# Four layers of graph attention on one core: layer 3 with stacked key terms, a one-pass leaky maximum, another step of lag, two copies on VectorE and a reordered step

## What is computed

```python
x = _layernorm(x + layer(x, adj))      # four times, another layer each time
```

```python
Wh = (h @ W).reshape(b, n, H, HD).transpose(0, 2, 1, 3)
e1 = jnp.einsum('bhnd,d->bhn', Wh, a1)
e2 = jnp.einsum('bhnd,d->bhn', Wh, a2)
e = e1[:, :, :, None] + e2[:, :, None, :]
e = jnp.where(adj_mask == 0, -jnp.inf, e)
e = jnp.where(e >= 0, e, 0.2 * e)
attn = jax.nn.softmax(e, axis=-1)
h_prime = jnp.einsum('bhij,bhjd->bhid', attn, Wh)
```

## Time and profile before

| | us |
|---|---|
| median of 3 runs | 723.36 (722.78 to 723.52) |
| profiled execution | 720.54 |
| its span, first to last instruction | 718.7 |
| TensorE busy | 653.0 (91%) |
| VectorE busy | 600.8 (84%) |
| ScalarE busy | 539.4 (75%) |
| GpSimd busy | 512.9 (71%) |

### The profile page before, as it was taken

One profiled execution on the slowest core, in us unless ns is written; L12 is line 12 of the kernel. 1 busy time (PEld: TensorE's weight loads), 2 busy tenths in 40 slices (PEclk: granted clock), 3 DMA queues, 4 the chain that ended last, 5 costly groups with the idle time before them and its releaser, 6 DMA issues.

```text
span 718.7 us, 17483 instructions
## 1 busy us (share of the span) xinstructions
PE 653.0 (91%) x6378; PEld 489.9 (68%) x6378; DVE 600.8 (84%) x1515; ACT 539.4 (75%) x852; POOL 512.9 (71%) x541
## 2 busy tenths in 40 slices
PE   3999799998799999999999998799999999999972
PEld 2888577776456666666666666676777777777751
DVE  4799679998778888988898886798888888888872
ACT  1555589987478777787777776588899899899882
POOL 6477559999675677767777765467776777767785
PEclk9999999999589999999999999999999999999996
DMA  9900000000000000000000000000100000100001
GB/s 255 279 3 1 2 0 1 2 1 2 0 1 2 3 1 2 1 2 1 2 2 2 2 1 2 1 2 1 31 16 16 16 17 16 31 16 16 16 16 44
DMA packets 28897, 14.91 MB, mean 21 GB/s; under 512 B 1926, under 2 KB 28812, under 8 KB 28812
## 3 DMA queue, kind: packets, MB, share of 16 engines
q1 hardware_dynamic: 25344, 12.59, 6.8%
q10 hardware_dynamic: 3468, 1.20, 0.8%
HBM read 9.59 MB, written 4.19 MB: 19 GB/s over the span
## 4 chain that ended last, share of the span: by engine, by line
PE 50%; DVE 18%; POOL 15%; issue 8%; POOLq 4%; ACT 4%; DMA 1%; DVEq 0%; ACTq 0%
PE pair L1083 15%; POOL arena L666 7%; PE pair L1269 5%; POOLq L527 4%; PE quad L1218 4%; DVE arena L993 3%; DVE nmx L999 3%; POOL yb L673 3%; POOL X L532 2%; PE quad L1136 2%; PE pair L1234 2%; PE pair L1248 2%; PE pair L1240 2%; POOL ln L526 2%; PE pair L1205 2%
## 5 line engine op out<-in xcount | busy, mean ns | idle before, releaser
L666 POOL TENSOR_TENSOR arena<-arena,nmx 128x1024 f32<-128x1024 f32 x64 | 121.3, 1896 | 74.0 <-DVE nmx L999 73.8
L644 POOL TENSOR_TENSOR arena<-arena,nmx 128x1024 f32<-128x1024 f32 x64 | 121.3, 1895 | 68.2 <-DVE nmx L1021 68.2
L1083 PE MATMUL pair<-identf,arena 128*128 128x128 f32 x1088 | 151.9, 282 | 0.9 <-DVE yb L1045 0.9
L1083 PEld LDWEIGHTS pair<-identf,arena 128*128 128x128 f32 x1088 | 118.1, 142 | 32.0 <-issue 31.0
L532 POOL TENSOR_SCALAR X<-yb,ln 128x128 f32<-128x128 f32 x256 | 113.7, 456 | 8.6 <-issue 8.6
L526 POOL TENSOR_TENSOR ln<-ln,neghalf 128x4 f32<-128x4 f32 x64 | 66.7, 1043 | 32.8 <-DVE ln L566 32.7
L792 ACT ACTIVATE arena<-quad 128x1024 f32<-128x1024 f32 x64 | 66.2, 1034 | 25.4 <-PE quad L1172 25.3
L1012 DVE TENSOR_TENSOR arena<-quad,mask 128x1024 f32<-128x1024 f32 x64 | 77.7, 1214 | 3.5 <-PE quad L1218 2.9
L1021 DVE TENSOR_REDUCE nmx<-arena 128x8 f32<-128x1024 f32 x64 | 78.0, 1218 | 1.8
L999 DVE TENSOR_REDUCE nmx<-arena 128x8 f32<-128x1024 f32 x64 | 78.0, 1218 | 1.7
L993 DVE TENSOR_TENSOR arena<-quad,arena 128x1024 f32<-128x1024 f32 x64 | 77.6, 1213 | 2.0 <-ACT arena L792 1.8
(11 more groups left out here) (190 smaller groups left out, 1431.9 us busy)
## 6 DMA issues: line engine op xcount, KB each, us to landing
X<-in_x SPq DMA_DIRECT2D x16, 256.0 KB, 5.5
arena<-in_adj SPq DMA_DIRECT2D x16, 256.0 KB, 5.6
out<-X SPq DMA_DIRECT2D x16, 256.0 KB, 2.3
nat_all<-in_L_gnn_W ACTq DMA_DIRECT2D x2, 64.0 KB, 5.3
w<-in_L_gnn_W ACTq DMA_DIRECT2D x2, 64.0 KB, 5.9
nat_all<-in_L_gnn_W_loop ACTq DMA_DIRECT2D x1, 64.0 KB, 2.7
nat_all<-in_L_gnn_Wg_loop ACTq DMA_DIRECT2D x1, 64.0 KB, 3.4
nat_all<-in_L_gnn_a ACTq DMA_DIRECT2D x1, 64.0 KB, 5.1
```

Source lines behind the costliest of these rows:

```text
L644: nc.gpsimd.tensor_tensor(v3(P2[t % 3], HEADS), v3(P2[t % 3], HEADS), nmx2[t % 2][:].unsqueeze(2).broadcast_to([128, HEADS, N]), ALU.add)\
L666: nc.gpsimd.tensor_tensor(v3(p, HEADS), v3(p, HEADS), nmx2[(t - 1) % 2][:].unsqueeze(2).broadcast_to([128, HEADS, N]), ALU.add)\
L1083: last = nc.tensor.transpose(dst[:, cols(i)], src[:, cols(i)], identf[:])
```

## The change

1. *Key terms stacked.* For graphs 1 to 3 of each batch the query and key terms come from one matmul of 512 columns. `ep` holds ones in eight more columns of each part, so `eT` has rows of ones, and a table `terms_of(b)` (in the room of `mask1`, free after layer 1) has the entries of `sel1` and, in the rows that meet the ones, the key terms of each head. SP fills the table: six copies of `sel1` once, and then for each batch eight small DMAs out of `eT`, each of three rows by three graphs by 128 elements. Graph 0 of a batch is as before.
2. *One-pass leaky maximum.* ScalarE makes relu(-0.8 s) in place of 0.2 s. VectorE then adds it to the scores and takes the row maximum in the same operation, eight times for the eight heads (`leaky_max`). GpSimd subtracts the maximum.
3. *One more step of lag* from the exponential on: exponential t-3, transposes t-4, values and output t-5, division t-6. The ring has five places. Two graphs of layer 3 instead of one have their slope and maximum inside layer 2's part of a step (`EARLY`).
4. *Copies.* VectorE copies `eT` (`terms_out`) and `vx` in place of ScalarE, but for the first batches. ScalarE's batch 1 values move to step 4.
5. *Statistics*, in all layers: one sum (variance + eps) where two small instructions stood; the scaling subtracts the mean itself.
6. *Order.* TensorE's output transposes stand ahead of the preparation. On VectorE `split_e` and the copy of the values stand behind the maximum, the copy of the terms ahead of it.

```diff
+LOWEST = -3e38
...
-AHEAD, BEHIND = 4, 13
-LAP, EARLY = 6, 1
+AHEAD, BEHIND = 4, 14
+LAP, EARLY = 6, 2
...
+        eps4 = sb("eps4", [128, G])
...
-        ln = [sb(f"ln{s}", [128, 3 * G]) for s in range(2)]
+        rstd = [sb(f"rstd{s}", [128, G]) for s in range(2)]
...
+        RING3 = [work[0][:], work[1][:], P2[1], P2[2], P2[0]]
...
+        def terms_of(b):
+            return mask1[:, bass.ts(b % 2, (G - 1) * HEADS * N)]
...
         def rows_of(t):
-            return P2[(t + GRAPHS) % 3]
+            return RING3[t % 5]
...
             general_sync(sp, read_flag(sp))
+            sp.wait_ge(sem("pool_ready"), 1)
+            sp.wait_ge(sem("L1_logits_mm"), BATCHES)
+            for i in range(2 * (G - 1)):
+                sp.dma_start(mask1[:, bass.ts(i, HEADS * N)], sel1[:]).then_inc(sem("L3_terms"), 16)
+            sp.wait_ge(sem("L3_terms"), 32 * (G - 1))
+
+            def terms(b):
+                sp.wait_ge(sem("L3_eT"), b + 1)
+                need(sp, sem("L3_s_mm"), G * (b - 1))
+                for h in range(HEADS):
+                    to = terms_of(b)[2 * HEADS + h:2 * HEADS + h + 65:32, :].rearrange("p (g c) -> p g c", g=G - 1)
+                    sp.dma_start(to[:, :, cols(h)], eT[b % 2][h:h + 65:32, D:].rearrange("p (g c) -> p g c", g=G - 1))                      .then_inc(sem("L3_terms"), 16)
+
+            for b in range(4):
+                terms(b)
             for b in range(BATCHES):
+                if real(b + 4):
+                    terms(b + 4)
                 sp.wait_ge(sem("L3_norm_done"), b + 1)
                 sp.dma_start(out[bass.ts(b, G)].rearrange("g n d -> n g d"), v3(x_of(b), G)).then_inc(sem("stored"), 16)
...
-            nc.gpsimd.tensor_tensor(ln[s][:, 2 * G:3 * G], ln[s][:, G:2 * G], neghalf[:], ALU.pow)
+            nc.gpsimd.tensor_tensor(rstd[s][:], rstd[s][:], neghalf[:], ALU.pow)
...
             for g in graphs:
-                last = nc.gpsimd.tensor_scalar(x_of(b)[:, cols(g)], y_of(L, b)[:, cols(g)], ln[s][:, g:g + 1],
-                                               ln[s][:, 2 * G + g:2 * G + g + 1], ALU.add, ALU.mult)
+                last = nc.gpsimd.tensor_scalar(x_of(b)[:, cols(g)], y_of(L, b)[:, cols(g)], mv[s][:, 2 * g:2 * g + 1],
+                                               rstd[s][:, g:g + 1], ALU.subtract, ALU.mult)
...
             m = v3(mv[s][:], G)
-            nc.vector.tensor_scalar(ln[s][:, 0:G], m[:, :, 0], -1.0, None, ALU.mult)
-            nc.vector.tensor_scalar(ln[s][:, G:2 * G], m[:, :, 1], EPS, None, ALU.add)\
-              .then_inc(sem(f"L{L}_stats_done"), 1)
+            nc.vector.tensor_tensor(rstd[s][:], m[:, :, 1], eps4[:], ALU.add).then_inc(sem(f"L{L}_stats_done"), 1)
...
-            nc.gpsimd.memset(ep[:], 0.0).then_inc(sem("pool_ready"), 1)
+            nc.gpsimd.memset(ep[:], 0.0).then_inc(sem("pool_set"), 1)
+            pool.wait_ge(sem("pool_set"), steps + 1)
+            nc.gpsimd.memset(ep[:].rearrange("p (g q c) -> p g q c", g=G, q=4)[:, :, 0:3, 2 * HEADS:3 * HEADS], 1.0)\
+              .then_inc(sem("pool_ready"), 1)
...
-                                            nmx2[(t - 1) % 2][:].unsqueeze(2).broadcast_to([128, HEADS, N]), ALU.add)\
+                                            nmx2[(t - 1) % 2][:].unsqueeze(2).broadcast_to([128, HEADS, N]), ALU.subtract)\
...
             def slope(t):
                 if graph(t):
                     act.wait_ge(sem("L3_s_mm"), t + 1)
-                    need(act, sem("L3_leaky"), t - 1)
-                    nc.scalar.mul(t3[t % 2], pair[t % 2], ALPHA).then_inc(sem("L3_scaled"), 1)
+                    need(act, sem("L3_max"), t - 1)
+                    nc.scalar.activation(t3[t % 2], pair[t % 2], ACT.Relu, scale=ALPHA - 1.0).then_inc(sem("L3_scaled"), 1)
...
+            def values_out(b):
+                act.wait_ge(sem("L3_v_mm"), b + 1)
+                need(act, sem("L3_pv_mm"), G * (b - 1))
+                nc.scalar.copy(vx[b % 2][:].rearrange("p (a c) -> p a c", c=HP)[:, :, 0:HD],
+                               v3(bank[6], G * HEADS)).then_inc(sem("L3_v"), 1)
+
             def layer3(t):
-                g = t - 4
+                g = t - 5
...
-                    if k == 2:
-                        act.wait_ge(sem("L3_eT_mm"), b + 1)
-                        need(act, sem("L3_s_mm"), G * (b - 1))
-                        nc.scalar.copy(eT[b % 2][:], bank[6].bitcast(BF16)[:, 0:W]).then_inc(sem("L3_eT"), 1)
-                    if k == 3:
-                        act.wait_ge(sem("L3_v_mm"), b + 1)
-                        need(act, sem("L3_pv_mm"), G * (b - 1))
-                        nc.scalar.copy(vx[b % 2][:].rearrange("p (a c) -> p a c", c=HP)[:, :, 0:HD],
-                                       v3(bank[6], G * HEADS)).then_inc(sem("L3_v"), 1)
+                if t == 4:
+                    values_out(1)
                 if t >= EARLY:
                     slope(t)
                 if graph(g):
                     act.wait_ge(sem("L3_pv_mm"), g + 1)
                     need(act, sem("L3_out_mm"), g - 1)
                     nc.scalar.copy(oT[g % 2][:], bank[7][:, 0:2 * N]).then_inc(sem("L3_oT"), 1)
-                if graph(t - 2):
-                    act.wait_ge(sem("L3_less_max"), t - 1)
-                    p = rows_of(t - 2)
+                if graph(t - 3):
+                    act.wait_ge(sem("L3_less_max"), t - 2)
+                    p = rows_of(t - 3)
                     nc.scalar.activation(p, p, ACT.Exp).then_inc(sem("L3_exp"), 1)
...
-            def leaky(t):
+            def terms_out(b):
+                dve.wait_ge(sem("L3_eT_mm"), b + 1)
+                need(dve, sem("L3_s_mm"), G * (b - 1))
+                nc.vector.tensor_copy(eT[b % 2][:], bank[6].bitcast(BF16)[:, 0:W]).then_inc(sem("L3_eT"), 1)
+
+            def leaky_max(t):
                 if graph(t):
                     p = rows_of(t)
-                    if t <= 2:
-                        dve.wait_ge(sem("L2_pT_mm"), GRAPHS - 2 + t)
+                    if 2 <= t <= 4:
+                        dve.wait_ge(sem("L2_pT_mm"), GRAPHS - 4 + t)
                     if t <= 1:
                         dve.wait_ge(sem("L2_less_max"), GRAPHS - 1 + t)
                     dve.wait_ge(sem("L3_scaled"), t + 1)
-                    need(dve, sem("L3_pT_mm"), t - 2)
-                    nc.vector.tensor_tensor(p, pair[t % 2], t3[t % 2], ALU.max).then_inc(sem("L3_leaky"), 1)
-
-            def row_max(t):
-                if graph(t):
-                    dve.wait_ge(sem("L3_leaky"), t + 1)
+                    need(dve, sem("L3_pT_mm"), t - 4)
                     need(dve, sem("L3_less_max"), t - 1)
-                    nc.vector.tensor_reduce(nmx2[t % 2][:], v3(rows_of(t), HEADS), AX.X, ALU.max, negate=True)\
-                      .then_inc(sem("L3_max"), 1)
+                    for h in range(HEADS):
+                        last = nc.vector.tensor_tensor_reduce(p[:, cols(h)], pair[t % 2][:, cols(h)], t3[t % 2][:, cols(h)],
+                                                              1.0, LOWEST, ALU.add, ALU.max, nmx2[t % 2][:, h:h + 1])
+                    last.then_inc(sem("L3_max"), 1)
 
             def layer2(t):
                 b, j = t // G, t % G
                 if GRAPHS <= t < GRAPHS + EARLY:
-                    leaky(t - GRAPHS)
-                    row_max(t - GRAPHS)
+                    leaky_max(t - GRAPHS)
+                if t == GRAPHS + 2:
+                    split_e(dve, 1, bank[6])
+                if t == GRAPHS + 3:
+                    terms_out(1)
...
             def layer3(t):
-                g = t - 5
+                g = t - 6
...
                 b, k = (t + AHEAD - 1) // G, (t + AHEAD - 1) % G
-                if k == 1 and real(b) and b > 0:
-                    split_e(dve, b, bank[6])
+                if k == 2 and real(b) and b > 1:
+                    terms_out(b)
                 b, j = t // G, t % G
                 if t > EARLY:
-                    leaky(t - 1)
+                    leaky_max(t - 1)
+                b, k = (t + AHEAD - 1) // G, (t + AHEAD - 1) % G
+                if k == 3 and real(b) and b > 1:
+                    dve.wait_ge(sem("L3_v_mm"), b + 1)
+                    need(dve, sem("L3_pv_mm"), G * (b - 1))
+                    nc.vector.tensor_copy(vx[b % 2][:].rearrange("p (a c) -> p a c", c=HP)[:, :, 0:HD],
+                                          v3(bank[6], G * HEADS)).then_inc(sem("L3_v"), 1)
+                if k == 1 and real(b) and b > 1:
+                    split_e(dve, b, bank[6])
+                b = t // G
                 if j == 3 and real(b - 2):
                     stats_done(dve, 3, b % 2)
-                if t > EARLY:
-                    row_max(t - 1)
                 if j in (1, 2) and real(b - 2):
                     stats_nodes(dve, 3, b - 2, b % 2, (2 * j - 2, 2 * j - 1))
...
-                need(pe, sem("L3_leaky"), t - 1)
+                need(pe, sem("L3_max"), t - 1)
```

(21 more changed lines are left out.)

3 lines of the change are left out of this document (2 added, 1 removed).

## The result

The kernel after took 736.23 us (median of 4 runs, 735.05 to 737.82), the kernel before 723.44 us beside it: a ratio of 1.018, 95% interval 1.016 to 1.020. It is slower by 12.8 us, where 712 us was forecast. The profiled execution of after took 737.82 us, its span is 736.1 us against 718.7.

A forecast was written before the change was run, and what follows sets the result against it. TensorE was taken to bind layer 3's steady part, VectorE 0.9 us a batch behind. Steady part -6.9, overlap -3.0, statistics -1.5 and lag 0 made -11.4 us off the median 723.36: 712 us, range 697 to 741.

The forecast's parts named there:

- part 4: Statistics, all layers: one VectorE instruction fewer, 0.08 us a batch, 1.5 us gained in layers 0 and 1; GpSimd hold uncounted.
- Part 1: Layer 3's stacked key terms: four key matmuls gone in three graphs, TensorE 1.3 us a batch less.
- Part 2: Layer 3's one-pass maximum on VectorE: eight operations at 0.29 us each, 0.6 us a batch cheaper than the old pair.
- rival B: Layer 3's maximum: accumulator free, slot near 0.21 us, TensorE binds again, 698 us; chance 0.15.
- Rival C: Slower through the slot of layer 3's eight maximum operations: 738 us at 0.35 us, 769 at 0.42; chance 0.27.
- Part 3: Layer 3's copies moved from ScalarE: VectorE 1.22 us a batch more; ScalarE 1.2 us freer, which buys nothing.
- VectorE's new batch: Layer 3's steady part: 14.6 us of work plus 0.35 gives 15.0 us, bound by VectorE, against 15.49; 6.9 us gained.
- rival E: Moved split and copies make TensorE and VectorE wait by turns, 0.5 to 0.8 us a batch: 719 to 723 us; chance 0.05.
- Part 5: Layer 3's extra step of lag: adds no wait in the steady part; 0 at the drain, +1.5 us as upper end.
- Part 6: Overlap of layers 2 and 3, 437 to 480 us: 3 us gained, range -6 to +2.
- Part 7: Layer 3's term DMAs: issues 0.31 us apart, 4.8 us at best against 6.4 available; hidden, 1.6 us to spare.
- Rival D: Layer 3's term DMAs come late, 9.6 us needed against 6.4, so batches wait: 743 us; chance 0.08.

The follow-up runs named there:

- e3: Kernel after, with the scaling's subtraction replaced by an addition, operands unmoved (doesn't compute the reference): 702.34 us, one run.
- e4: Kernel after, with the two old statistics instructions and old operand tile, but the scaling still subtracting (doesn't compute the reference): 739.74 us, one run.
- e1: Kernel after, with the old statistics back: two small VectorE instructions, GpSimd scaling by add and multiply; 707.38 us, ratio 0.978 to the kernel before.
- e2: Kernel before, with only the new statistics and the subtract, multiply scaling: 763.83 us, ratio 1.055 to the kernel before.
- e7: e1 with the key terms of all four graphs unstacked and no term DMAs: 712.80 us, ratio 0.988 to the kernel before.
- e9: e1 with the copies of key terms and values back on ScalarE: 719.40 us, ratio 0.996 to the kernel before.
- e6: Kernel after, with GpSimd adding eps and negating the means, scaling by add, multiply; VectorE stops at the aggregates: 706.98 us, ratio 0.976 to before.
- e8: e1 with the leaky maximum in two VectorE passes and ScalarE's multiply back: 738.29 us, ratio 1.022 to the kernel before.
- e5: Kernel after, keeping VectorE's one sum, with GpSimd negating the means and scaling by add, multiply: 704.57 us, ratio 0.975 to the kernel before.

## Why the prediction was wrong

**The step that failed is part 4, statistics.** It counted VectorE's one instruction less in all layers (-1.5 us) and put the same edit's other half at nothing, without a reason: the scaling on GpSimd, 256 instructions, changed its pair of operations. It costs 358 ns more each. The start of layer 3 came 30.5 us later where I had 1.5 us earlier. e3 and e4 show the cause, e1 and e2 its size. The 1.5 us don't show either: e3 keeps the single sum and reaches the first mark at 438.0 us, where the kernel before has 438.1. The part also looked for the holder in layers 0 and 1 among VectorE and TensorE; GpSimd had only 0.58 us a batch to spare in layer 0 and 0.46 in layer 1, and no row of the prediction showed its waits there.

**Part 1** was right in its rows (four key matmuls gone in three graphs, start to start of the banks 0.43 us: 597.04 to 597.47) and half right in its worth: 7 us by e7, which is 0.6 us a batch of the 1.3.

**Part 2** had the slot at 0.29 us; it is 0.21. The lower bound was the right row, the 128-column sum at the same shape, and what I added to it, the accumulator's read, runs beside the next operation. The Trainium skill ("VectorE: DVE Perf Modes", section on two Vector instructions with no wait between them) says that there are two instructions, and the trace shows both. The prediction's estimate of 0.133 + 2 x 0.075 = 0.283 us, with the 75 ns of the "Vector Engine (DVE) Microarchitecture Reference" (section 5.2) taken twice, is not what the queue is held for: it is held for 0.21 us, as if they were paid once. So rival B's slot holds, and its 698 us are near what the new layer 3 gives when the scaling adds (702.3 us in e3). Rival C falls: that its 738 us, for a slot of 0.35 us, stand near the measured 736 is chance.

**Part 3**: the copies hold VectorE 0.33 us (604.23 to 604.56) and 0.60 us (595.74 to 596.34), 0.93 a batch where I had 1.22. That ScalarE's relief buys nothing is refuted by e9: beside the extra lag it is worth 13 us, through the wait ahead of the values' copy.

**Part 4's hold**: the one small instruction is held 1.45 us, as the first of the pair was at 468.54, and now in the steady part too. "SBUF — State Buffer" of the Trainium skill (section "SBUF: two separate sides") says a Vector instruction with two SBUF inputs is locked out like a two-port one; row 606.87 agrees for the two-input sum. e1's first small instruction, with one input, is held alike: 1.2 to 1.5 us in 14 of layer 3's 16 batches. But not every GpSimd instruction holds the sum: in layer 0 of the kernel after it took 0.18 us (at 57.36) while GpSimd scaled 128x128 rows out of SBUF (57.08 to 59.75). Taken away from VectorE, the hold gave 0.15 us a batch back before the term DMAs became the next wait (e6).

**VectorE's new batch** came out near the forecast by luck, by errors against each other: 14.63 us where I had 15.0. The slot gave 32 x 0.08 = 2.6 us back, the hold took 1.3, and the rest is waits. Nor is VectorE alone the bound. e7 shows TensorE at 15.21 us without idle time, so 13.9 us in e1; e8 shows VectorE at 16.69, so at most 16.69 - 4 x (2.4 - 1.7) = 13.9 us too. Both need 13.9 at most and the batch is 14.6, so 0.7 us a batch are waits of one for another. That is near rival E's mechanism, on top of rival B's slot, but E named two engines and there are three: in 540 to 620 us of e1 VectorE waits 5.3 us for GpSimd and 1.7 for TensorE, TensorE 2.2 for VectorE and 1.4, once, for a DMA. Which of these waits sets the batch, no run shows.

**Part 5** had the sign right: no gain in the steady part, 1 to 3 us lost where I had 0 to 1.5. It said that the lag adds no wait; it would have added one to the values' copy, had that stayed on ScalarE (e9).

**Part 6**: -5.1 us where I had -3.0. e3 shows it over the same stretch as the earlier trace rows, since it starts layer 3 when the kernel before does: the granted clock of 437 to 480 us is 1.00, where it was 0.96, and from the first graph's scores to the tenth's it takes 38.7 us instead of 44.0, where I had 41.

**Part 7** was right in effect and wrong in size: hidden, but the issues start 0.75 us apart, and the 1.6 us to spare are gone. 8 x 0.75 = 6.0 us of issues end at 610.65 and the terms are taken at 611.88, 7.2 us after the copy ends at 604.64, where I had 6.4. The last one lands within 2.0 us of its issue, under the 2.3 that I took as the best. (My worst, 6.0 us, isn't the worst landing of that view; it has one of 6.4.) Rival D's lateness is the next wait once the hold is gone: e6 found it.

**The sum.** Forecast -1.5, -3.0, -6.9, 0 for start, overlap, steady part and end; e3, the change without its subtraction, has -0.1, -5.1, -12.0, -0.8 by the marks (span 700.6). With it, +30.5, -5.1, -9.1, +1.2. That 736 us lies in the range is luck: the range reached so far for the slot and the DMAs (rivals C and D), and neither cost the time.

## What to carry to other kernels

An algebraic rewrite that saves an instruction on one engine has to be priced on every engine that reads its result: here x - mean for x + (-mean) cost GpSimd 358 ns in each of 256 instructions. Before an engine is called idle enough, its waits are to be read in every stage, not its share of the page: GpSimd was 71% busy and had 0.58 us to spare where the batch is 3.6 us. And a copy's cost in a queue isn't only its duration. It's also the wait that it stands in, with all that is queued behind it, and a change of lag elsewhere can make that wait.

## What the runs showed of the hardware

- GpSimd's tensor-scalar instruction on 128x128 float32: add, multiply 456 to 462 ns (before, e1, e3, e5); subtract, multiply 814 to 818 ns (after, e2, e4), whichever tile the operands come from. The subtraction of two tensors (128x1024) shows no such difference: 1.90 us in the kernel after, by subtract, and 1.90 in layer 2, by add.
- VectorE's one-pass operation with an accumulator, 128 columns: starts 0.21 us apart, with the accumulator's read of 83 ns beside the next operation.
- A DMA issue of nine pieces (2.2 KB) from SP: 0.70 us, starts 0.75 apart, where one of 256 KB takes 0.42.
- A small instruction on VectorE (128x4) lasts up to 1.45 us when it starts 0.47 us after GpSimd's subtraction of 128x1024, and ends with it, with one SBUF input (e1) as with two (after). Beside GpSimd's scaling of 128x128 it takes 0.18 us.
